# Decoder block with routed experts: results added to token rows block by block, all dense groups ahead of the expert blocks

## The chip, the cores and the metric

One core of a Trainium2 chip runs the whole layer. A core has five engines that run their own instruction streams and meet at semaphores: TensorE (PE, matrix products and transposes), VectorE (DVE), ScalarE (ACT), GpSimd (POOL), and SyncE (SP), which here only issues DMAs. GpSimd issues DMAs too, those that gather or scatter rows by an index. The metric is device time in microseconds, the median of three runs; smaller is better.

## The reference, cut to what matters

The input x is 4 sequences of 1024 tokens of 256 numbers, in float32. The layer is a causal linear attention with 16 heads, a cross attention over 77 context rows, and a feed-forward part with one shared network and eight experts. 512 of the tokens (index_b, index_t) go to the experts:

```
x = x + linear_attention(layernorm(x))
x = x + cross_attention(layernorm(x), ctx)
h = layernorm(x)
shared = ln(silu(h @ sw1.T + sb1) * (h @ sw2.T + sb2)) @ sw3.T + sb3        # all 4096 tokens
h_moe  = h[index_b, index_t]                                              # 512 tokens
e      = argmax(sigmoid(h_moe @ eg_w.T + eg_b) + exp_bias)
w      = softmax([sigmoid(h_moe @ sg_w.T + sg_b), score of e])
y      = ln(silu(h_moe @ ew1[e].T + eb1[e]) * (h_moe @ ew2[e].T + eb2[e])) @ ew3[e].T + eb3[e]
shared[index_b, index_t] = shared[index_b, index_t] * w[0] + y * w[1]
out = x + shared
```

## The kernel before, in words

The 4096 tokens are 32 tiles of 128 (NT), in 8 groups of 4 (NG, GT). A loop of 36 steps does both attentions, tile by tile, in a software pipeline; each finished tile of x is also stored to a scratch tensor in DRAM called rows. The loop's last steps already begin with the feed-forward part.

The feed-forward part goes by units, in the order of the tuple UNITS (L43): F0 to F4, G0, F5, F6, M0, M1, M2, F7. An F unit is a dense group, four tiles through the shared network. G is the gathered group, the 512 tokens that go to the experts, fetched by index from rows and sent through the shared network, for their share of it and for the routing. M units are the experts' blocks: the 512 tokens are sorted by expert into 11 blocks of 128 rows (NBLK), each with rows of one expert only, the last rows of an expert's blocks empty; M0 and M1 have four blocks, M2 three. Every engine runs the loop `for q in range(3, ...)`, and does in step q parts of units q-2 to q+2: on TensorE the gate products of unit q (L688), the transposes of its gated features z for unit q-1 (L721), the input transposes of unit q+1 (L661), and the output products y of unit q-1 (L739). With q = GATHERED = 5 stands G, with FIRST_M = 8 stands M0.

Around the change the order is this.

- GpSimd scatters the normalized gathered tokens into the sorted area of rows (L1666, q = 5) by slot_u; SP loads the blocks back (L441). It also does half of the dense groups' normalizations (norm_h3, L1545), adds the output bias to a whole dense group (bias_tiles, L1560, 128x1024), and computes inverse deviations (invert_variance, L1570; invert_blocks, L1583).
- VectorE writes the gated features (gated, L1231: first an instruction over two SBUF operands, L1235, then one with a PSUM operand, L1240), takes their variances, and evicts y (y_evict, L1210): an F unit is added to x, which SP stores to the output; of an M unit's blocks two are copied by VectorE and two by ScalarE (L989) into ys, and SP stores them to rows (store_ys, L429).
- For the gathered tokens VectorE computes the mixing weights (weigh, L1390, q = 6; weights, L1398, q = 7), then g_a = x + w[0] * shared (add_shared, L1405), to which it adds w[1] * eb3[e] (add_expert_bias, L1410) in q = 8 and 9, from products that TensorE makes (gathered_bias, L796).
- At the end GpSimd gathers the 512 results from rows by slot (L1673), VectorE adds w[1] * result to g_a (add_expert, L1418), and, once every dense group is stored to the output (out_stored), GpSimd scatters the four tiles over it (L1677).

Of the kernel before, what the change touches and what calls it, by code (L numbers as in the profile page):

```python
# [13 lines left out]
P = 128  # L14
# [29 lines left out]
         + tuple(("M", k) for k in range(NMG)) + (("F", NG - 1),))  # L44
# [5 lines left out]
BIAS_ROWS = 64 + NE  # L50

# [6 lines left out]
def decoder_block(nc, A):  # L58
    ctx = ExitStack()
    with ctx:  # L60
# [115 lines left out]
        def qkc(slot, ch):  # L176
# [25 lines left out]
        ys = wide_[:, 2816:5632].rearrange("p (b d) -> p b d", b=NBLK)  # L202
        g_x2, g_sh, hg, g_a = (wide_[:, n:n + 1024].rearrange("p (m d) -> p m d", m=MT)
                               for n in (5632, 6656, 7680, 11264))
        m_th, m_u, m_z = (wide_[:, n:n + 512].rearrange("p (j n) -> p j n", j=GT) for n in (9728, 10240, 10752))
        g_ys, g_out = x[:, 0:MT, :], x[:, MT:2 * MT, :]
        zeros = sb("zeros", [P, D])
# [84 lines left out]
        elog_done, oht_ready, mth_ready, mzt_ready, pair_exp, hg_scaled, ys_copied = (  # L292
            sem(f"act_g_{n}") for n in ("elog", "oht", "mth", "mzt", "pair", "hg", "ys"))
        (idx_ready, cols_ready, g_stat, g_agg, logit_ready, gate_chain, onehot_ready, pair_ready,
         rank_read, slot_ready, block_ready, mu_ready, mz_ready, mstat_done, mzmv_ready, mzn_ready, ys_ready, gsh_ready,
         ga_ready, gb_ready, gout_ready) = (
            sem(f"dve_g_{n}") for n in ("idx", "cols", "stat", "agg", "logit", "gate", "onehot", "pair",
                                        "rank_read", "slot", "block", "mu", "mz", "mstat", "mzmv", "mzn", "ys", "gsh",
                                        "ga", "gb", "out"))
# [4 lines left out]
        ys_stored = sem("ys_stored")  # L304
        gathered = sem("gathered")
        gathered_ys = [sem(f"gathered_ys{m}") for m in range(MT)]
# [11 lines left out]
        ys_v = rows_2[(NT + NBLK) * P:(NT + 2 * NBLK) * P, :].rearrange("(b p) d -> p b d", p=P)  # L318
        to_hs = rows_2[0:(NT + NBLK) * P, :]
        from_ys = rows_2[0:(NT + 2 * NBLK) * P, :]  # L320
# [43 lines left out]
        def _(sp):  # L364
# [52 lines left out]
            load(hs_v, zeros[:, :].unsqueeze(1).to_broadcast([P, NBLK, D]), zeroed)  # L417
# [11 lines left out]
            def store_ys(k):  # L429
                b = blocks_of(k)  # L430
                sp.wait_ge(ys_ready, 2 * (k + 1))
                sp.wait_ge(ys_copied, min(2 * (k + 1), NBLK - 2 * NMG))
                sp.dma_start(ys_v[:, b.start:b.stop, :], ys[:, b.start:b.stop, :]).then_inc(ys_stored, 16)

            for n, (what, k) in enumerate(UNITS):

                if n == 3:
                    sp.wait_ge(placed, 16 * MT)
                    for m in range(NMG):
                        b = blocks_of(m)  # L440
                        sp.dma_start(hs_in[:, b.start:b.stop, :], hs_v[:, b.start:b.stop, :]).then_inc(hs_loaded[m], 16)  # L441
                if what == "F":
                    store_out(k)
                if what == "M":
                    store_ys(k)
            sp.wait_ge(out_stored, 16 * (NG + 1))
            sp.wait_ge(scattered, 16 * MT)
# [3 lines left out]
        def _(pe):  # L451
# [287 lines left out]
            def y_products(pe, n, expert=None):  # L739
                if not 0 <= n < NU:  # L740
                    return
                if is_dense(n):
                    wait(pe, x1_ready, NT)
                    wait(pe, den_ready, NG)
                    wait(pe, ktok_ready, NT)
                    wait(pe, pt_ready, NT)
                    wait(pe, z_ready, dense(n) + 1)
                else:
                    wait(pe, mzt_ready, UNITS[n][1] + 1)
                wait(pe, out_ready, GT * ahead(n, "F"))  # L750
                wait(pe, gsh_ready, GT * ahead(n, "G"))
                wait(pe, ys_ready, 2 * ahead(n, "M"))
                wait(pe, ys_copied, min(2 * ahead(n, "M"), NBLK - 2 * NMG))
# [81 lines left out]
            for q in range(3, NU + 1):  # L835
                if q == FIRST_M - 1:
                    pe.wait_ge(block_ready, 1)
                for half in range(2):
                    gate_products(pe, q, half, expert, load_expert if FIRST_M - 1 <= q < NU - 1 else None)
# [14 lines left out]
        def _(act):  # L854
# [133 lines left out]

            def evict_ys(n):  # L989
                if is_moe(n):  # L990
                    for j in range(2, size(n)):
                        wait(act, y_done, rows_ahead(n) + size(n))
                        copy(ys[:, GT * UNITS[n][1] + j, :], bank[2][:, (j % 2) * D:(j % 2 + 1) * D]).then_inc(ys_copied, 1)

# [31 lines left out]
            for q in range(3, NU + 1):  # L1026
                evict_ys(q - 2)
# [18 lines left out]
        def _(dve):  # L1046
# [307 lines left out]
            def choose_slots():  # L1354
# [17 lines left out]
                dve.tensor_scalar(slot_y[:, :], slot_f[:, :], float(NBLK * P), None, ALU.add).then_inc(slot_ready, 1)  # L1372
# [25 lines left out]
            def weights():  # L1398
                dve.wait_ge(pair_exp, 1)
                then_wait(dve.tensor_reduce(pair_sum[:, :], pair_e[:, :, :], mybir.AxisListType.X, ALU.add))  # L1400
                then_wait(dve.reciprocal(pair_r[:, :], pair_sum[:, :]))
                then_wait(dve.tensor_tensor(mix[:, :, :], pair_e[:, :, :],
                                            pair_r[:, :].unsqueeze(2).to_broadcast([P, MT, 2]), ALU.mult))

            def add_shared(m):  # L1405
                dve.wait_ge(gsh_ready, m + 1)
                dve.scalar_tensor_tensor(out=g_a[:, m, :], in0=g_sh[:, m, :], scalar=mix[:, m, 0:1], in1=g_x2[:, m, :],
                                         op0=ALU.mult, op1=ALU.add).then_inc(ga_ready, 1)

            def add_expert_bias(half):  # L1410
                dve.wait_ge(gbe_done, half + 1)
                for j in range(2):
                    m = 2 * half + j
                    dve.wait_ge(ga_ready, m + 1)
                    dve.scalar_tensor_tensor(out=g_a[:, m, :], in0=bank[3][:, j * D:(j + 1) * D], scalar=mix[:, m, 1:2],
                                             in1=g_a[:, m, :], op0=ALU.mult, op1=ALU.add).then_inc(gb_ready, 1)

            def add_expert(m):  # L1418
                dve.wait_ge(gathered_ys[m], 16)
                dve.wait_ge(gb_ready, m + 1)  # L1420
                dve.scalar_tensor_tensor(out=g_out[:, m, :], in0=g_ys[:, m, :], scalar=mix[:, m, 1:2], in1=g_a[:, m, :],
                                         op0=ALU.mult, op1=ALU.add).then_inc(gout_ready, 1)
# [43 lines left out]
            for q in range(3, NU + 2):  # L1466
# [18 lines left out]
                if q in (FIRST_M, FIRST_M + 1):  # L1485
                    add_expert_bias(q - FIRST_M)
            for m in range(MT):
                add_expert(m)
# [3 lines left out]
        def _(pool):  # L1492
# [129 lines left out]
            pool.memset(zeros[:, :], 0.0)  # L1622
# [27 lines left out]
            for q in range(3, NU + 1):  # L1650

                if q == GATHERED - 2:
# [7 lines left out]
                elif q == GATHERED:  # L1660
# [14 lines left out]
            for m in range(MT):  # L1675
# [61 lines left out]
```

## Time and profile before

| | before |
|---|---|
| median of 3 runs | 413.1 us (413.07 to 413.27) |
| the profiled execution | 412.16 us, of which 410.4 us are the span that the profile shows |
| busy TensorE / VectorE / ScalarE / GpSimd | 375.3 / 299.5 / 166.2 / 252.1 us |
| mean granted clock of TensorE | 0.986 of full speed |
| attention loop, about | 40 to 300 us |
| feed-forward units, about | 300 to 397 us |
| from TensorE's last product to the end of the span | 396.5 to 410.4 us |

The span is the time between the first and the last instruction or transfer of one execution. Busy times of different engines overlap, so that they don't add up to it. What bounds a stretch is read from who waits for whom in that stretch.

### The profile page before, as it was taken

Reading aid. Unit: us, or ns where it says so; the run is one execution under the profiler, and the core shown is the slowest. Engines: PE = TensorE matmul, PEld = TensorE weight load, DVE = VectorE, ACT = ScalarE, POOL = GpSimd, SP = SyncE. Lnnn points to the kernel's source line nnn. Section 1 sums busy time; section 2 is a strip of 40 time slices with the busy share of each in tenths; the row PEclk is TensorE's granted clock in tenths of the full one; section 3 lists DMA queues with packets and bytes.
Section 4 is the critical chain, followed back from the end, with each engine's and each line's share of the span. In section 5 each row is a group of like instructions: output and inputs, shape, how many; then the busy total and the mean of one; then the engine's idle time right before and its main releaser. Section 6 shows DMA issues by size and latency. Waiting matters only on the chain. (4 is left out here: it accounts for less than half of the span.)

```text
span 410.4 us, 11152 instructions
## 1 busy us (share of the span) xinstructions
PE 375.3 (91%) x3826; PEld 259.3 (63%) x3826; DVE 299.5 (73%) x930; ACT 166.2 (41%) x401; POOL 252.1 (61%) x382
## 2 busy tenths in 40 slices
PE   7989899999999999999999999999799979979950
PEld 3455567766776777767767666677566646567630
DVE  2646778888878888888887788785654667988641
ACT  3171343454355344435335424433365443234410
POOL 5133855666656665676656676588788776823435
PEclk9999999999999999999999999999999999999995
DMA  7982591300210120030020012012000320353233
GB/s 225 336 263 51 130 340 53 66 27 14 44 39 25 24 60 14 16 79 15 15 58 22 28 28 53 15 30 65 28 14 27 109 96 2 110 186 103 68 102 126
DMA packets 35743, 31.88 MB, mean 78 GB/s; under 512 B 4027, under 2 KB 34632, under 8 KB 35688
## 3 DMA queue, kind: packets, MB, share of 16 engines
q1 hardware_dynamic: 33160, 26.42, 22.6%
q0 software_dynamic: 1120, 3.36, 2.8%
q10 hardware_dynamic: 1408, 1.39, 1.0%
q8 instruction: 32, 0.52, 0.6%
q14 instruction: 23, 0.19, 0.1%
HBM read 14.64 MB, written 12.32 MB: 66 GB/s over the span
## 5 line engine op out<-in xcount | busy, mean ns | idle before, releaser
L1515 POOL TENSOR_TENSOR s_t<-s_t,causal 128x512 f32<-128x512 f32 x64 | 80.2, 1274 | 75.5 <-ACT s_t L856 75.5
L465 PE MATMUL bank<-h1t,w_qkv 128*128 128x512 f32 x112 | 55.4, 617 | 1.0 <-DVE x L1101 0.8
L1137 DVE TENSOR_TENSOR s_t<-sbank,causal 128x512 f32<-128x512 f32 x64 | 40.8, 678 | 0.0
L472 PE MATMUL bank<-w_qkv,h1t 128*128 128x256 f32 x128 | 35.9, 403 | 2.3 <-DVE arena L1057 2.2
L856 ACT ACTIVATE s_t<-sbank 128x512 f32<-128x512 f32 x64 | 34.2, 587 | 9.1 <-PE sbank L486 9.1
L526 PE MATMUL bank<-s_t,vp 128*32 128x128 f32 x1024 | 34.6, 275 | 2.5 <-DVE s_t L1137 0.9
L486 PE MATMUL sbank<-arena 32*128 32x256 f32 x512 | 36.7, 400 | 0.0
L1101 DVE TENSOR_TENSOR x<-bank,x 128x256 f32<-128x256 f32 x32 | 13.6, 424 | 30.2 <-PE bank L605 30.1
L698 PE MATMUL sbank<-h1t,w 128*128 128x512 f32 x72 | 33.0, 596 | 0.5 <-ACT h1t L856 0.5
L605 PE MATMUL bank<-w_out,attn_t 128*128 128x256 f32 x128 | 33.1, 381 | 0.0
L1523 POOL TENSOR_TENSOR rr<-ve,neg_half 128x3 f32<-128x3 f32 x36 | 31.0, 861 | 3.0
L526 PEld LDWEIGHTS bank<-s_t,vp 128*32 128x32 f32 x1024 | 26.3, 109 | 9.7 <-issue 9.7
L1123 DVE BATCH_NORM_STATS2 stats<-x 128x6 f32<-128x256 f32 x87 | 31.6, 412 | 0.5 <-issue 0.5
L912 ACT ACTIVATE prob<-sc,nmx 128x77 f32<-128x77 f32 x32 | 11.5, 360 | 48.0 <-DVE nmx L1157 48.0
L465 PEld LDWEIGHTS bank<-h1t,w_qkv 128*128 128x128 f32 x112 | 19.0, 189 | 18.1 <-issue 13.7
L856 ACT ACTIVATE prob_t<-bank 77x128 f32<-77x128 f32 x32 | 8.7, 272 | 50.8 <-PE bank L453 50.8
L1057 DVE TENSOR_SCALAR arena<-bank,b_qk 128x512 f32<-128x512 f32 x28 | 21.0, 750 | 11.3 <-PE bank L465 11.3
L856 ACT ACTIVATE k_tok<-bank 128x256 f32<-128x256 f32 x32 | 12.2, 383 | 40.8 <-PE bank L453 40.8
L472 PEld LDWEIGHTS bank<-w_qkv,h1t 128*128 128x128 f32 x128 | 21.8, 189 | 8.8 <-DVE arena L1057 6.7
L486 PEld LDWEIGHTS sbank<-arena 32*128 32x128 f32 x512 | 23.1, 184 | 3.9 <-issue 2.4
L453 PE MATMUL bank<-ident,h 128*128 128x128 f32 x128 | 24.0, 273 | 1.6 <-ACT h L863 1.5
L1534 POOL TENSOR_TENSOR x<-x,b_out 128x256 f32<-128x256 f32 x32 | 23.4, 730 | 0.0
(215 smaller groups left out, 809.7 us busy)
## 6 DMA issues: line engine op xcount, KB each, us to landing
rden_t<-rden SPq DMA_DIRECT2D x64, 64.0 KB
rows<-x SPq DMA_DIRECT2D x32, 128.0 KB, 1.7
x<-in_x SPq DMA_DIRECT2D x7, 512.0 KB, 7.4
out<-x SPq DMA_DIRECT2D x7, 512.0 KB
we<-in_we SPq DMA_DIRECT2D x1, 2048.0 KB
rows<-zeros SPq DMA_DIRECT2D x1, 1408.0 KB, 7.1
xmask<-in_mask POOLq DMA_DIRECT2D x2, 616.0 KB, 7.9
we<-in_we SPq DMA_DIRECT2D x1, 1024.0 KB
```

The costliest lines, as they stand in the source:

```text
L453: return pe.transpose(dst, src, ident[:, :])
L465: mm = pe.matmul(dst[:, :], w_qkv[:, ch, cb * P:(cb + 1) * P], h1t[:, g % 3, ch, :], start=(ch == 0), stop=(ch == CH - 1))
L472: mm = pe.matmul(bank[0][:, 0:D], h1t[:, (t // GT) % 3, ch, tok(t)], w_qkv[:, ch, 2 * D:3 * D], start=(ch == 0), stop=(ch == CH - 1))
L486: mm = pe.matmul(both, kt(slot, ch)[rows, tok(t)], qpair(slot, ch)[rows, :, tok(t)], start=True, stop=True)
L526: mm = pe.matmul(bank[3][32 * r:32 * r + 32, ch * P:(ch + 1) * P], v_of, s_t[:, r, 2 * ch + par, :], start=(first and ch + par == 0), stop ...
L605: mm = pe.matmul(bank[0][:, 0:D], attn_t[:, M % 2, ch, :], w_out[:, ch, :], start=(ch == 0), stop=(ch == CH - 1))
L698: mm = pe.matmul(sbank[2 + half][:, :], w_12[:, ch, half * HF:(half + 1) * HF], h3t[:, n % 2, ch, :], start=(ch == 0), stop=(ch == CH - 1))
L856: return act.activation(dst, src, ACT.Copy)
L1123: last = dve.bn_stats(stats[:, k, :], x[:, t, :])
L1137: dve.tensor_tensor(s_t[:, r, :, :], sbank[r][:, :].rearrange("p (s q) -> p s q", s=4), causal[:, :].unsqueeze(1).to_broadcast([P, 4, P]), ...
L1515: pool.tensor_tensor(s_t[:, r, :, :], s_t[:, r, :, :], causal[:, :].unsqueeze(1).to_broadcast([P, 4, P]), ALU.mult)\
L1523: pool.tensor_tensor(rr[:, i, :], ve[:, i, :], neg_half[:, 0:3], ALU.pow).then_inc(rr_ready, 1)
```

## The change

The dense group F7 goes ahead of the experts' blocks in UNITS, so that M0, M1 and M2 come last (FIRST_M is now 9, and M2 is unit 11). The experts' results no longer go through DRAM. Instead the sums g_a (x plus the shared part plus the expert's bias), with two more columns, the token's weight w[1] and its index in the output, are scattered by GpSimd into a sorted area of rows with 258 columns (place_bases, behind q = 8), which SP had filled beforehand, during tile 16, with zeros and an index out of range (NOWHERE). SP loads them back by unit into res (load_base, behind F7's output store). VectorE then evicts y as res = y * weight + res, all four blocks itself, and GpSimd scatters each block from res to the output by the index column, with a bounds test that skips the empty rows (scatter_blocks, one unit's blocks at the head of steps 11, 12 and 13). The step q = 6 on GpSimd has an order of its own: inverse deviation of G, then the bias of F5 and F6. The experts' bias is added in q = 7 and 8.

```diff
-         + tuple(("M", k) for k in range(NMG)) + (("F", NG - 1),))
+         + (("F", NG - 1),) + tuple(("M", k) for k in range(NMG)))
+BW = D + 2
+BASE_AT = -(-(NT + NBLK) * P * D // BW)
+NOWHERE = 2 * NB * S
             for t in range(NT):
                 if t % GT == 1 and t // GT + 1 < NG:
                     spread(t // GT + 1)
+                if t == 2 * TPB:
+                    load(base_v, empty[:, :].unsqueeze(1).to_broadcast([P, NBLK, BW]), emptied)
-            def store_ys(k):
+            def load_base(k):
                 b = blocks_of(k)
-                sp.wait_ge(ys_ready, 2 * (k + 1))
-                sp.wait_ge(ys_copied, min(2 * (k + 1), NBLK - 2 * NMG))
-                sp.dma_start(ys_v[:, b.start:b.stop, :], ys[:, b.start:b.stop, :]).then_inc(ys_stored, 16)
+                sp.wait_ge(based, 16 * MT)
+                sp.dma_start(res[:, b.start:b.stop, :], base_v[:, b.start:b.stop, :]).then_inc(base_loaded[k], 16)
@@ tensor
-                if q in (FIRST_M, FIRST_M + 1):
-                    gathered_bias(pe, q - FIRST_M)
+                if q in (GATHERED + 2, GATHERED + 3):
+                    gathered_bias(pe, q - GATHERED - 2)
@@ scalar
-                evict_ys(q - 2)
@@ vector, y_evict
+                if is_moe(n):
+                    k = UNITS[n][1]
+                    b = blocks_of(k)
+                    dve.wait_ge(base_loaded[k], 16)
+                    dve.tensor_copy(token_u[:, b.start:b.stop], res[:, b.start:b.stop, D + 1]).then_inc(token_ready, 1)
-                    elif j < 2:
-                        dve.tensor_copy(ys[:, GT * UNITS[n][1] + j, :], y).then_inc(ys_ready, 1)
+                    else:
+                        b = GT * UNITS[n][1] + j
+                        dve.scalar_tensor_tensor(out=res[:, b, 0:D], in0=y, scalar=res[:, b, D:D + 1], in1=res[:, b, 0:D],
+                                                 op0=ALU.mult, op1=ALU.add).then_inc(ys_ready, 1)
@@ vector, weights
+                dve.tensor_copy(g_a[:, :, D], mix[:, :, 1]).then_inc(meta_ready, 1)
+                dve.tensor_copy(g_a[:, :, D + 1], idx_f[:, :]).then_inc(meta_ready, 1)
@@ vector, add_expert and its calls are gone; add_expert_bias in q of 7 and 8
@@ gpsimd
+            def place_bases():
+                pool.wait_ge(emptied, 16)
+                pool.wait_ge(meta_ready, 2)
+                for m in range(MT):
+                    pool.wait_ge(gb_ready, m + 1)
+                    pool.indirect_dma_start(out=to_base, out_offset=bass.IndirectOffsetOnAxis(slot_y[:, m:m + 1], 0),
+                                            in_=g_a[:, m, :], in_offset=None).then_inc(based, 16)
+            def scatter_blocks(n):
+                if is_moe(n):
+                    k = UNITS[n][1]
+                    pool.wait_ge(token_ready, k + 1)
+                    pool.wait_ge(out_stored, 16 * (NG + 1))
+                    for b in blocks_of(k):
+                        pool.wait_ge(ys_ready, b + 1)
+                        pool.indirect_dma_start(out=A["out"], out_offset=bass.IndirectOffsetOnAxis(token_u[:, b:b + 1], 0),
+                                                in_=res[:, b, 0:D], in_offset=None, bounds_check=NB * S - 1,
+                                                oob_is_err=False).then_inc(scattered, 16)
-            for q in range(3, NU + 1):
+            for q in range(3, NU + 2):
+                scatter_blocks(q - 2)
...
                                                 in_=hg[:, m, :], in_offset=None).then_inc(placed, 16)
+                elif q == GATHERED + 1:
+                    norm_h3(q + 2)
+                    invert_variance(q - 1)
+                    bias_tiles(q)
                     bias_tiles(q + 1)
                 else:
                     at(q)
-            pool.wait_ge(ys_stored, 16 * NMG)
-            for m in range(MT):
-                gather(m, g_ys, from_ys, slot_y, gathered_ys[m])
-            pool.wait_ge(out_stored, 16 * (NG + 1))
-            for m in range(MT):
-                pool.wait_ge(gout_ready, m + 1)
-                pool.indirect_dma_start(out=A["out"], out_offset=bass.IndirectOffsetOnAxis(idx_u[:, m:m + 1], 0),
-                                        in_=g_out[:, m, :], in_offset=None).then_inc(scattered, 16)
+                if q == GATHERED + 3:
+                    place_bases()
```

## Rows read from the trace of the kernel before

**Rows 1.** Stretches: from:to, length, busy time (and count) per engine, clock, DMA, GB/s
```profile
400.00:405.00 5.00, 0.00 (x0) 0.00 (x0) 1.85 (x4) 0.00 (x0) 3.46 (x4) 0.50 0.60 188
```

**Rows 2.** Chain that ended last, from 396 us: start, length, what
```profile
398.76 3.91 DMA out<-x
```

**Rows 3.** Timeline of GpSimd, the tail: start, length, instruction [idle before, releaser]
```profile
397.17 1.07 POOL L1601 DMA_INDIRECT x<-rows,slot_y  x1 [0.20 <-issue]
...
404.24 1.09 POOL L1677 DMA_INDIRECT out<-x,idx_u  x1 [0.30 <-issue]
405.64 0.97 POOL L1677 DMA_INDIRECT out<-x,idx_u  x1 [0.30 <-issue]
406.91 0.97 POOL L1677 DMA_INDIRECT out<-x,idx_u  x1 [0.30 <-issue]
```

**Rows 4.** Timeline of TensorE, from the gathered group on
```profile
359.78 1.06 PE L453 MATMUL sbank<-ident,arena 128*128 128x128 f32 x8 [1.15 <-DMA arena<-rows]
362.43 1.97 PE L759 MATMUL bank<-w_3c,s_t 128*128 128x256 f32 x8 [1.59 <-DVE arena L1226]
...
371.27 1.13 PE L800 MATMUL bank<-be,onehot_t 8*128 8x256 f32 x4
...
378.10 1.99 PE L759 MATMUL bank<-we,s_t 128*128 x8 [0.30 <-ACT s_t L999]
...
387.56 3.60 PE L698 MATMUL sbank<-h1t,w 128*128 128x512 f32 x8
390.99 0.49 PE L453 MATMUL bank<-ident,arena 128*128 128x128 f32 x3
...
394.54 1.97 PE L759 MATMUL bank<-w_3c,s_t 128*128 128x256 f32 x8 [0.21 <-ACT arena L856]
```

**Rows 5.** Timeline of VectorE, the same stretch
```profile
348.48 0.19 DVE L1369 TENSOR_TENSOR place<-place,onehot 128x32 f32<-128x32 f32 x1
...
355.08 4.06 DVE L1391 TENSOR_TENSOR oh_score<-onehot,score 128x32 f32<-128x32 f32 x1
...
360.63 1.66 DVE L1226 SCALAR_TENSOR_TENSOR arena<-bank,z_r,y_bias 128x256 f32<-128x256 f32 x4 [0.67 <-POOL z_r L1581]
362.20 0.68 DVE L1235 SCALAR_TENSOR_TENSOR s_t<-s_t 128x512 f32<-128x512 f32 x1
362.97 0.75 DVE L1240 SCALAR_TENSOR_TENSOR s_t<-sbank,b,s_t 128x512 f32<-128x512 f32 x1
...
365.29 1.67 DVE L1407 SCALAR_TENSOR_TENSOR arena<-arena,mix 128x256 f32<-128x256 f32 x4
...
375.25 1.19 DVE L1271 TENSOR_SCALAR arena<-arena,g_zmv,m_r 128x128 f32<-128x128 f32 x4
```

**Rows 6.** Timeline of GpSimd, from the gathered group on
```profile
354.43 4.65 POOL L1567 TENSOR_TENSOR x<-x,y_bias 128x1024 f32<-128x1024 f32 x2
359.17 0.23 POOL L1574 TENSOR_SCALAR z_ve<-z_mv 128x4 f32<-128x4 f32 x1
359.48 1.04 POOL L1581 TENSOR_TENSOR z_r<-z_ve,neg_half 128x4 f32<-128x4 f32 x1
...
387.00 0.86 POOL L1591 TENSOR_TENSOR m_r<-m_ve,neg_half 128x3 f32<-128x3 f32 x1
```

**Rows 7.** Timelines of GpSimd and VectorE near 298 and 305 us
```profile
298.63 0.55 POOL L1529 TENSOR_SCALAR h<-x,nm,rr 128x256 f32<-128x256 f32 x1
...
305.35 1.06 POOL L1529 TENSOR_SCALAR h<-x,nm,rr 128x256 f32<-128x256 f32 x1
...
305.45 0.69 DVE L1235 SCALAR_TENSOR_TENSOR s_t<-s_t 128x512 f32<-128x512 f32 x1
```

**Rows 8.** DMA: the block loads' issues in ns, their time to landing, and the issues' table
```profile
L441 SPq DMA_DIRECT2D arena<-rows x3: 367/507/508, 355.9 to 356.8; - x3
...
DMA to landing us min/median/max: 3.8/4.8/6.2
...
rows<-zeros SPq DMA_DIRECT2D x1, 1408.0 KB, 7.1
```

More of the change, by code:

```diff
@@ L201, in decoder_block @@
         hs_in = wide_[:, 0:2816].rearrange("p (b d) -> p b d", b=NBLK)
[L202 to L207, printed above, removed]
+        res = wide_[:, 2816:2816 + NBLK * BW].rearrange("p (b d) -> p b d", b=NBLK)
+        g_x2, g_sh, hg = (wide_[:, n:n + 1024].rearrange("p (m d) -> p m d", m=MT) for n in (5632, 6656, 7680))
+        g_a = wide_[:, 8704:8704 + MT * BW].rearrange("p (m d) -> p m d", m=MT)
+        m_th, m_u, m_z = (wide_[:, n:n + 512].rearrange("p (j n) -> p j n", j=GT) for n in (9792, 10304, 10816))
+        empty = sb("empty", [P, BW])
+        token_u = sb("token_u", [P, NBLK], U32)
         ones16 = sb("ones16", [P, P], BF16)
@@ L291, in decoder_block @@
             sem(f"pe_g_{n}") for n in ("logit", "rank", "oht", "mxa", "mztr", "gbe"))
-        elog_done, oht_ready, mth_ready, mzt_ready, pair_exp, hg_scaled, ys_copied = (
-            sem(f"act_g_{n}") for n in ("elog", "oht", "mth", "mzt", "pair", "hg", "ys"))
+        elog_done, oht_ready, mth_ready, mzt_ready, pair_exp, hg_scaled = (
+            sem(f"act_g_{n}") for n in ("elog", "oht", "mth", "mzt", "pair", "hg"))
         (idx_ready, cols_ready, g_stat, g_agg, logit_ready, gate_chain, onehot_ready, pair_ready,
          rank_read, slot_ready, block_ready, mu_ready, mz_ready, mstat_done, mzmv_ready, mzn_ready, ys_ready, gsh_ready,
-         ga_ready, gb_ready, gout_ready) = (
+         ga_ready, gb_ready, meta_ready, token_ready) = (
             sem(f"dve_g_{n}") for n in ("idx", "cols", "stat", "agg", "logit", "gate", "onehot", "pair",
                                         "rank_read", "slot", "block", "mu", "mz", "mstat", "mzmv", "mzn", "ys", "gsh",
-                                        "ga", "gb", "out"))
+                                        "ga", "gb", "meta", "token"))
         h3_pooled, g_ve, g_nr, hg_ready, mve_ready, mr_ready = (
@@ L303, in decoder_block @@
         hs_loaded = [sem(f"hs_loaded{k}") for k in range(NMG)]
-        ys_stored = sem("ys_stored")
         gathered = sem("gathered")
-        gathered_ys = [sem(f"gathered_ys{m}") for m in range(MT)]
+        emptied, based = sem("emptied"), sem("based")
+        base_loaded = [sem(f"base_loaded{k}") for k in range(NMG)]
         scattered = sem("scattered")
@@ L416, in _ @@
             load(idx_t[:, :], A["idx_t"], w_moe_in)
-            load(hs_v, zeros[:, :].unsqueeze(1).to_broadcast([P, NBLK, D]), zeroed)
+            load(hs_v, empty[:, 0:D].unsqueeze(1).to_broadcast([P, NBLK, D]), zeroed)
             for t in range(NT):
@@ L444, in _ @@
                 if what == "M":
-                    store_ys(k)
+                    load_base(k)
             sp.wait_ge(out_stored, 16 * (NG + 1))
-            sp.wait_ge(scattered, 16 * MT)
+            sp.wait_ge(scattered, 16 * NBLK)
         @block.tensor
@@ L751, in y_products @@
                 wait(pe, gsh_ready, GT * ahead(n, "G"))
-                wait(pe, ys_ready, 2 * ahead(n, "M"))
-                wait(pe, ys_copied, min(2 * ahead(n, "M"), NBLK - 2 * NMG))
+                wait(pe, ys_ready, min(GT * ahead(n, "M"), NBLK))
                 for j in range(size(n)):
@@ L838, in _ @@
                 for half in range(2):
-                    gate_products(pe, q, half, expert, load_expert if FIRST_M - 1 <= q < NU - 1 else None)
+                    gate_products(pe, q, half, expert, load_expert if FIRST_M - 1 <= q < NU else None)
                 z_features(pe, q - 1)
@@ L986, in gates @@
                     act.activation(m_th[:, own, :], x1, ACT.Tanh, scale=0.5).then_inc(mth_ready, 1)
[L989 to L993, printed above, removed]
             def evict_z(n):
@@ L1371, in choose_slots @@
                 dve.tensor_copy(slot_u[:, :], slot_f[:, :]).then_inc(slot_ready, 1)
-                dve.tensor_scalar(slot_y[:, :], slot_f[:, :], float(NBLK * P), None, ALU.add).then_inc(slot_ready, 1)
+                dve.tensor_scalar(slot_y[:, :], slot_f[:, :], float(BASE_AT - NT * P), None, ALU.add)\
+                    .then_inc(slot_ready, 1)
             def map_blocks():
@@ L1403, in weights @@
                                             pair_r[:, :].unsqueeze(2).to_broadcast([P, MT, 2]), ALU.mult))
+                dve.tensor_copy(g_a[:, :, D], mix[:, :, 1]).then_inc(meta_ready, 1)
+                dve.tensor_copy(g_a[:, :, D + 1], idx_f[:, :]).then_inc(meta_ready, 1)
             def add_shared(m):
                 dve.wait_ge(gsh_ready, m + 1)
-                dve.scalar_tensor_tensor(out=g_a[:, m, :], in0=g_sh[:, m, :], scalar=mix[:, m, 0:1], in1=g_x2[:, m, :],
+                dve.scalar_tensor_tensor(out=g_a[:, m, 0:D], in0=g_sh[:, m, :], scalar=mix[:, m, 0:1], in1=g_x2[:, m, :],
                                          op0=ALU.mult, op1=ALU.add).then_inc(ga_ready, 1)
@@ L1414, in add_expert_bias @@
                     dve.wait_ge(ga_ready, m + 1)
[L1415 to L1422, printed above, removed]
+                    dve.scalar_tensor_tensor(out=g_a[:, m, 0:D], in0=bank[3][:, j * D:(j + 1) * D], scalar=mix[:, m, 1:2],
+                                             in1=g_a[:, m, 0:D], op0=ALU.mult, op1=ALU.add).then_inc(gb_ready, 1)
             def first_stats_of(lo, hi):
@@ L1621, in _ @@
             pool.memset(one1[:, :], 1.0)
-            pool.memset(zeros[:, :], 0.0)
+            pool.memset(empty[:, 0:BW - 1], 0.0)
+            pool.memset(empty[:, BW - 1:BW], float(NOWHERE))
             pool.memset(vp[:, :, :, :], 0.0)
```

11 lines of the change are left out of this document (5 added, 6 removed).

## The prediction, made before the changed kernel was run

> **What bounds the kernel now.** I read the stretches first, then the chain of waits, then the engines' timelines from 350 us on. Up to 396 us TensorE is hardly ever idle; from 400 to 405 it does nothing and the DMA share is 0.60 [rows 1]. The span therefore ends with a tail that no matmul covers. The last dense group's store holds it for 3.91 us [rows 2], and GpSimd issues four gathers and four scatters by index, each 0.96 to 1.09 us and 0.30 us apart [rows 3]. The last scatter ends at 407.88 and the span at 410.4, so its landing costs 2.5. Ahead of the tail, TensorE waits twice in the gathered group's neighbourhood: 1.15 us for the sorted tokens, and 1.59 us for the vector engine [rows 4].
>
> The second of these waits has a cause one engine further on. A 128x32 product on VectorE takes 4.06 us at 355.08, while one of the same shape and both operands in SBUF takes 0.19 at 348.48 [rows 5]. It ends at 359.14, where GpSimd's two 128x1024 bias sums end (354.43 + 4.65 = 359.08) [rows 6]. Only then can the mixing weights go on.
>
> **The change, part by part.** Times below are on the clock of the profiled execution: its span is 410.4, 1.76 more lie around it (412.16), and the median of the runs is 0.94 above that (413.1).
>
> *Tail removed.* Gone are three stores of results, four gathers, four final sums and four scatters to the output. After TensorE's last product (396.5) they and the last group's evictions took 13.9 us to the end.
>
> *F7 moved ahead of the blocks.* Its TensorE work is the same: 3.43 us of gate products (387.56 to the next at 390.99), 1.98 of output products [rows 4], 1.3 of transposes, 6.7 in all. The blocks start that much later unless idle time goes. The 1.15 us wait for sorted tokens goes: F7's transposes now stand there, and their input (two GpSimd normalizations, 0.55 each [rows 7], behind the placement scatters, after which GpSimd is free at 354.4 [rows 6]) is ready at 355.5.
>
> *GpSimd's order.* The gathered group's inverse deviation now goes ahead of the bias sums: ready at 355.5 + 0.09 + 0.20 + 0.08 + 1.04 = 356.9, where it was 360.5 [rows 6]. The group's four evictions (1.66 [rows 5]) end at 358.6 instead of 362.2, so the 1.59 us wait goes too. Were that all, 2.7 us of TensorE's idle time would go.
>
> But the bias sums are now three in a row (F5, F6 and, because F7 has moved up, F7), 2.35 each: 356.9 to 363.9. At 358.6 VectorE comes to the gate's first product of unit 7, 128x512 with both inputs in SBUF. The row at 355.08 says what such an instruction does when it meets back-to-back bias sums: it waited through the rest of both. The hold works the other way too: a 0.55 us normalization on GpSimd took 1.06 while VectorE's product of that form ran [rows 7]. So I let it wait until 363.9, then 0.68 + 0.75 [rows 5] gives z at 365.4.
>
> The Trainium skill, "SBUF — State Buffer", section "SBUF: two separate sides", says that GpSimd and a VectorE instruction with two SBUF inputs exclude each other over a shared port pair, and whichever starts first keeps it for the whole instruction. By that rule alone the product would get in after the first or second sum (359.3 or 361.6); the trace's 4.06 us shows a wait over two.
>
> From there, unit by unit (VectorE in program order):
> - VectorE: z 365.4; variance of unit 6 to 366.4; weights and the two new small copies to 367.3 (0.57 before, 0.3 taken for the copies, from the 0.16 to 0.19 of small instructions); four sums of the shared part to 368.9 (1.67); half of the experts' biases 0.8 (halves of the 1.66 rows) to 369.7; F5 out 1.6 to 371.3 [rows 5].
> - TensorE: y of unit 6 from 359.4, bias products 1.06 to 362.3, then waits 3.1 for z; F7's gates 365.4 to 368.9; transposes; waits 1.1 for F5 out; y 371.4 to 373.2, bias products to 374.2. M0's gates start at 374.2, which was 364.2 before: 10.0 later, 3.3 more than F7's 6.7.
> - M0 as before, 8.2 without the wait, then the last dense group's variance (after M0's, as in the program) ends at 381.6; GpSimd's two inverses (1.4, 1.3 [rows 6]) put F7's scale at 383.0 and M0's at 384.3; F7 is out at 384.6, M0's normalization ends at 385.8 (1.19 [rows 5]), and 1.74 later, as before (376.36 to 378.10 [rows 4]), its y products run to 389.5. M2's gates end at 392.6, 8.2 later than before.
>
> *The experts' bias* is added two units earlier, so g_a is ready at 375.1. Four placement scatters follow at 1.27 (0.97 + 0.30 [rows 3]): 375.2 to 380.3, landed by 383. Queued behind them on GpSimd is the inverse for F7, which wants nothing before 381.6: hidden, by 1.3 us.
>
> *Emptying the base rows* during tile 16 is a 1.45 MB store; the like one landed in 7.1 us [rows 8]. The tile after it stores its rows a whole tile step (8.4 us) later and nobody waits for those: nothing, and at worst about 1 us once. The second memset (0.1) lies in GpSimd's idle 1.1 us at the start: nothing.
>
> *Base rows back to SBUF.* Nothing like this load stood in the tail. SP issues it behind F7's store: 384.7 + two issues of 0.5 = about 385.2. Lower bound 3.8, upper 6.2 to landing for the three comparable loads, median 4.8 [rows 8]; 3.91 for a 256 KB store in contention [rows 2]. I take 5.0, as 512 KB of store are ahead: 390.2. M0's products are done at 389.5, so this load holds by 0.7, and could hold by 2.
>
> *Evictions and scatters.* VectorE: a small copy and 0.45, first block at 390.8; GpSimd starts at 391.1. Now 11 scatters instead of four, with a bounds test and rows skipped: no row shows one. Bounds: the skipped rows (896 of 1408) may cost nothing, 0.3 + 0.35 x 0.97 = 0.65 each; the test may add to the slowest spacing 1.40 (404.24 to 405.64 [rows 3]); 1.6 is my estimate of the most, one and a half times as far above that as it is above 1.27. I take 1.27, the spacing of plain ones. M0's four end at 396.2; M2's inverse is queued behind them (0.20 + 0.08 + 0.86 + gaps = 1.2; its input is there at 395.6) to 397.4; seven more to 406.3, of which the last 0.3 is gap. M2's own results are evicted from 400.9 on, before its scatters' turn at 402.5. End: 406.0 + 2.5 = 408.5, against 410.4: 1.9 saved. So 410.3 for a profiled execution, 411.2 for the median.
>
> **The rivals.**
> (B) VectorE gets in between bias sums. At 361.6 everything behind is 2.1 us earlier: 409.1; if it is never held, M0 starts 4.1 earlier: 407.1. For: the 0.09 us gap ahead of a small GpSimd instruction let VectorE in at 359.1 [rows 6], and the third sum comes from another step of the program. Against: two sums already ran without such a gap.
> (C) Scatters get cheap with their skipped rows. At 0.65 the tail is no longer GpSimd's; it is gates of M2 (392.6) + 8.3 to the first eviction + three scatters + landing: about 405.6, so 408.3.
> (D) Slower: the bounds test costs more than skipped rows give. GpSimd's queue holds 11 scatters in a row on the path, so each 0.1 costs 1.1. From 1.27 + 1.9/11 = 1.44 there is no gain, above 1.52 it is slower; at 1.6 it is 3.6 more: 414.8. For: 1.40 has been seen among plain ones, and these are issued behind waits. Against: most rows move nothing.
> (E) The base load lands 2 us later behind F7's store (6.2 and more instead of 5): 413.1, no change. This is also how the edit could fail to do what it says: one wait for a DMA replaced by another.
>
> **How the numbers follow.** Forecast 0.45 (411.2, by itself 409.7 to 412.6), B 0.18, C 0.12, D 0.15, E 0.10. The range reaches from B's end to short of D's: 406.8 to 414.0. What this kernel's measurement can tell from no change is 0.2%, 0.8 us. Faster is below 412.3: most of the forecast's case (0.39), B, C: 0.69. Same: the forecast's rest 0.05, most of E, D's edge: 0.14. Slower: D and some of E: 0.17.
>
> **What would show it.** In the trace after: three bias sums end near 364 and a 128x512 product on VectorE takes about 5.3 us; if it takes 0.7, B. TensorE starts M0's gates at 374. A load of base rows lands within 1 us of M0's last product. Eleven output scatters 1.27 apart (C, D by their spacing), the first at 391, and after TensorE's last product (401) about 7.5 us to the end instead of 13.9. The forecast is wrong if the product isn't held, if the spacing is not near 1.27, or if GpSimd's queue is not what ends last.

## The result, and the profile after

The changed kernel takes 410.01 us (median of 20 runs, 407.03 to 413.65) beside 414.95 for the kernel before (20 runs, 411.46 to 416.9, the first three of which are those shown ahead of the prediction). The ratio is 0.988, with an interval of 0.985 to 0.991: 5.0 us faster (3.8 to 6.3). The forecast was 411.2 with 1.9 us saved. The time lies in the range, but the saving is more than twice the forecast one. That 410.01 comes so near to 411.2 is in part luck: the forecast stood on 413.1, the median of three runs of the kernel before, and over 20 runs that median is 1.9 higher.

In the profiled executions the span went from 410.4 to 406.6 us. Executions of one kernel differ ahead of the stretch that was changed (last section), so I compare traces by what comes after one instruction that no edit touches: the start of TensorE's output products of unit 5, the gathered group, at 352.79 before and 353.02 after. Put on the clock of the trace before, the span after is 406.6 - 0.23 = 406.4, 4.0 us less.

TensorE's timeline after, from the gathered group on:

```profile
358.70 1.04 PE L460 MATMUL sbank<-ident,h1t 128*128 128x128 f32 x8
359.57 1.89 PE L765 MATMUL bank<-w_3c,s_t 128*128 128x256 f32 x8
361.39 1.12 PE L806 MATMUL bank<-be,onehot_t 8*128 8x256 f32 x4
362.45 3.70 PE L705 MATMUL sbank<-h1t,w 128*128 128x512 f32 x8
...
369.11 1.96 PE L765 MATMUL bank<-w_3c,s_t 128*128 128x256 f32 x8 [1.65 <-DVE x L1226]
371.00 1.12 PE L806 MATMUL bank<-be,onehot_t 8*128 8x256 f32 x4
372.06 1.13 PE L718 MATMUL sbank<-we,h1t 128*128 x4
```

Both waits of [rows 4] in this stretch (1.15 and 1.59 us) are gone, and F7's gates follow at 362.45 without a wait, where the forecast had 3.1 us of idleness. One wait of 1.65 us is new, for F5's evictions. M0's gates start at 372.06; the forecast said 374.2.

VectorE and GpSimd in the same stretch, two fences that answer to [rows 5] and [rows 6]:

```profile
355.32 0.15 DVE L1397 TENSOR_TENSOR oh_score<-onehot,score 128x32 f32<-128x32 f32 x1
...
357.32 1.66 DVE L1229 SCALAR_TENSOR_TENSOR arena<-bank,z_r,y_bias 128x256 f32<-128x256 f32 x4 [0.86 <-POOL z_r L1581]
358.90 1.21 DVE L1240 SCALAR_TENSOR_TENSOR s_t<-s_t 128x512 f32<-128x512 f32 x1
...
362.32 2.33 DVE L1408 TENSOR_TENSOR mix<-pair_e,pair_r 128x8 f32<-128x8 f32 x1
...
367.20 1.65 DVE L1226 SCALAR_TENSOR_TENSOR x<-bank,z_r,x 128x256 f32<-128x256 f32 x4
```

```profile
356.18 1.04 POOL L1581 TENSOR_TENSOR z_r<-z_ve,neg_half 128x4 f32<-128x4 f32 x1
357.21 7.42 POOL L1567 TENSOR_TENSOR x<-x,y_bias 128x1024 f32<-128x1024 f32 x3
```

The three bias sums stand back to back as forecast (end 364.63). But the gate's first product, which comes at 358.90, takes 1.21 us and not 5.3: it is through at 360.11. The three sums take 7.42 instead of three times 2.35, the second of them 2.80, since it had to wait for the product. The weights' product (8 numbers for each partition), ready at 362.32, is then held through the third sum, 2.33 us instead of the 0.17 that it took before. It came 0.04 us too late; the third sum in the chain of waits:

```profile
362.28 2.34 POOL x L1567
```

A stretch of the chain that ended last, and the timeline of GpSimd's tail, which answers to [rows 2] and [rows 3]:

```profile
383.28 4.32 DMA arena<-rows
387.63 0.04 DVE token_u L1215
```

```profile
389.11 1.05 POOL L1667 DMA_INDIRECT out<-arena,token_u  x1 [0.80 <-DVE arena L1233]
...
394.36 0.88 POOL L1591 TENSOR_TENSOR m_r<-m_ve,neg_half 128x3 f32<-128x3 f32 x1
395.45 1.10 POOL L1667 DMA_INDIRECT out<-arena,token_u  x1 [0.20 <-issue]
...
401.96 0.97 POOL L1667 DMA_INDIRECT out<-arena,token_u  x1 [0.31 <-issue]
403.23 0.97 POOL L1667 DMA_INDIRECT out<-arena,token_u  x1 [0.30 <-issue]
```

The load of M0's base rows (first fence) takes 4.32 us and lands at 387.60, when M0's products are done (385.53 + 1.99 = 387.5). The 11 scatters are 1.27 to 1.40 apart, but for M2's inverse between the first four and the rest. The last is issued by 404.20 and its landing takes 2.4.

### The profile page after: what moved, and what is told of

Read it like the earlier page. It is cut to its first block and busy times, and to the rows that moved or that the text cites. A ratio compares the mean times of both kernels' runs of the same rounds, so it can differ in the third digit from the quotient of the medians.

```text
span 406.6 us, 11163 instructions
## 1 busy us (share of the span) xinstructions
PE 375.4 (92%) x3826; PEld 259.2 (64%) x3826; DVE 298.8 (73%) x936; ACT 164.8 (41%) x396; POOL 259.6 (64%) x390
```

## Experiments

The aligned span in the table is the profiled span less the delay of unit 5's output products against 352.79. h1_small_product has no ratio: it was executed once, as were h2_small_between and h3_product_later, which are told of below. The other ratios rest on 6 to 20 runs of a kernel.

| run | edit | span | aligned | ratio to before (95% interval) |
|---|---|---|---|---|
| before | | 410.4 | 410.4 | |
| after | the change | 406.6 | 406.4 | 0.988 (0.985 to 0.991) |
| c0_changed | the change again | 408.4 | 406.6 | 0.990 (0.984 to 0.995) |
| u1_units_only | before, F7 ahead of the blocks | 418.7 | 416.7 | 1.014 (1.010 to 1.018) |
| p1_inverse_first | before, GpSimd's new step 6 | 410.0 | 408.3 | 0.992 (0.989 to 0.995) |
| b1_bias_late, b2 | after, F7's bias sum late | 404.4, 406.1 | 404.3, 404.3 | 0.985 (0.981 to 0.990), 0.986 (0.980 to 0.992) |
| n1_no_skip | after, all rows written | 408.4 | 406.4 | 0.989 (0.983 to 0.994) |
| t1_seven | after, without M0's scatters | 405.2 | 405.2 | 0.986 (0.980 to 0.992) |
| h1_small_product | after, one product more | 406.2 | 406.2 | |
| f1_bias_late_base_first, f2 | b1, base rows first | 408.7, 405.7 | 403.8, 403.9 | 0.980 (0.975 to 0.985), 0.987 (0.981 to 0.993) |

**The change again (c0_changed).** No edit.

> The changed kernel once more, beside the others: about 0.988 of the kernel before. Its trace tells whether the 4.06 us hold of a small two-input product on VectorE and the short waits of the changed kernel (1.21 and 2.33 us for instructions of 0.68 and 0.17) come out alike in every execution. If VectorE gets in between two bias sums by chance, the numbers differ from run to run; if it depends on the order of the instructions, they repeat.

The holds repeat to 0.01 us: 1.22 and 2.33. The third sum starts 0.04 us ahead of the weights' product here too (363.90 and 363.94). So they come from the program, the order of its instructions and their times, and not from chance.

**The order of the units alone (u1_units_only).**

```diff
 # before.py
-         + tuple(("M", k) for k in range(NMG)) + (("F", NG - 1),))
+         + (("F", NG - 1),) + tuple(("M", k) for k in range(NMG)))
-                    gate_products(pe, q, half, expert, load_expert if FIRST_M - 1 <= q < NU - 1 else None)
+                    gate_products(pe, q, half, expert, load_expert if FIRST_M - 1 <= q < NU else None)
-            for q in range(3, NU + 1):        # ScalarE, for evict_ys
+            for q in range(3, NU + 2):
```

> The kernel before with F7 moved ahead of the blocks and nothing else. Theory 1 (the gain needs the results' new way to the output): slower than before by about 3 us, since store of M2's results (2.5 to landing), four gathers (1.27 apart, 3.6 to landing), four sums and four scatters now all stand behind TensorE's last product with nothing beside them: last product near 397, end near 413. Theory 2 (the order of the dense groups alone brings the gain, by the idle 1.15 us and 1.59 us on TensorE): 2 to 3 us faster than before.

Slower by 1.4%, 6.3 us in the aligned span: theory 1's sign, at twice its size. The end is what it says, one after the other. The chain of waits from 403 us:

```profile
403.43 2.51 DMA rows<-arena
...
406.22 1.06 POOL x L1601
...
411.35 1.00 POOL out L1677
...
415.22 0.97 POOL out L1677
```

The rest of its loss is in the gathered group. GpSimd now has F7's normalizations between its two bias sums, and the small product is held through all of them:

```profile
357.12 5.14 DVE L1391 TENSOR_TENSOR oh_score<-onehot,score 128x32 f32<-128x32 f32 x1
```

```profile
356.47 2.35 POOL L1567 TENSOR_TENSOR x<-x,y_bias 128x1024 f32<-128x1024 f32 x1
358.80 1.09 POOL L1557 TENSOR_SCALAR h1t<-x,nm,rr 128x256 f32<-128x256 f32 x2
359.87 2.34 POOL L1567 TENSOR_TENSOR x<-x,y_bias 128x1024 f32<-128x1024 f32 x1
```

TensorE then waits 4.01 us where it waited 1.59 before. So the order of the units is not a gain by itself: in the changed kernel it pays together with the results' new way and GpSimd's new order. What it would bring with only one of them was not run.

**GpSimd's order of step 6 alone (p1_inverse_first).**

```diff
 # before.py
+                elif q == GATHERED + 1:
+                    norm_h3(q + 2)
+                    invert_variance(q - 1)
+                    bias_tiles(q)
+                    bias_tiles(q + 1)
```
(the bias sum of F5 goes from step 5 to here)

> The kernel before with only GpSimd's order of step 6 changed (the gathered group's inverse deviation ahead of the two bias sums). Theory 1 (the hold is what TensorE waits for): the small product takes 0.2 us instead of 4.06, the gathered group's evictions end near 359, TensorE's wait of 1.59 us at 362.43 goes and its blocks start 1.6 to 1.8 us earlier; time 1.6 us less. Theory 2 (the tail is set by something that does not move, the store of F7 and the gathers): less than 0.4 us.

```profile
356.76 0.15 DVE L1391 TENSOR_TENSOR oh_score<-onehot,score 128x32 f32<-128x32 f32 x1
```

```profile
362.43 1.89 PE L759 MATMUL bank<-w_3c,s_t 128*128 128x256 f32 x8
```

Theory 1: the small product takes 0.15 us, TensorE's wait of 1.59 is gone, the aligned span is 2.1 us less and the ratio 0.992. By the traces this order alone brings about half of what the change brings (2.1 of 4.0); the two ratios' intervals (0.992, 0.988) meet. The tail does not take it back.

**F7's bias sum late (b1_bias_late, b2_bias_late).**

```diff
 # after.py, GpSimd
+                elif q == GATHERED + 2:
+                    norm_h3(q + 2)
+                    invert_variance(q - 1)
+                    pool.wait_ge(ga_ready, MT)
+                    bias_tiles(q + 1)
```

> The changed kernel with F7's bias sum moved behind the inverse deviation of unit 6 and behind VectorE's sums of the shared part. Theory 1: the weights' product (2.33 us at 362.3) takes 0.17, F5's evictions end near 366.7 instead of 368.8, TensorE's wait of 1.65 us at 369.1 goes and M0's gates start near 370.3; everything behind moves with it, so 1.6 to 2 us less than the changed kernel. Theory 2: the bias sum in its new place holds another VectorE instruction with two SBUF inputs (the gate's first product of unit 8) for as long, and nothing is won.

> The changed kernel with the late bias sum, again, beside the next one on one chip: 2 us less than the changed kernel, 0.985 to 0.987 of the kernel before.

VectorE of b1_bias_late, and TensorE's start of M0:

```profile
362.20 0.17 DVE L1408 TENSOR_TENSOR mix<-pair_e,pair_r 128x8 f32<-128x8 f32 x1
...
364.94 1.64 DVE L1226 SCALAR_TENSOR_TENSOR x<-bank,z_r,x 128x256 f32<-128x256 f32 x4
366.50 0.72 DVE L1240 SCALAR_TENSOR_TENSOR s_t<-s_t 128x512 f32<-128x512 f32 x1
```

```profile
370.04 1.13 PE L718 MATMUL sbank<-we,h1t 128*128 x4
```

The product is no longer held (0.17), M0 starts 2.0 us earlier (1.9 aligned) and the end comes 2.1 us earlier in both traces. Against the changed kernel the ratios (0.985 and 0.986, beside 0.988 and 0.990) point the same way, but their intervals overlap. The third sum ahead of this work was on the path; theory 2 is out, as the gate's product at 366.50 took 0.72. But the edit moves two things: with the hold goes the wait of F5's inverse deviation behind that sum, which F5's evictions need (ready at 366.19 before the edit, at 363.59 with it). Had only the hold gone, the evictions would have started near 366.2 instead of 367.2, by my estimate from these rows. So about 1 us of the 2.1 is the hold's alone, and the rest needs the earlier inverse too.

**No row skipped (n1_no_skip).** Every scatter writes its 128 rows to a scratch tensor of its own; the experts' tokens are missing from the output.

```diff
 # after.py
-                        pool.indirect_dma_start(out=A["out"], ...
-                                                in_=res[:, b, 0:D], in_offset=None, bounds_check=NB * S - 1,
-                                                oob_is_err=False).then_inc(scattered, 16)
+                        pool.indirect_dma_start(out=A[f"dump{b}"], ...
+                                                in_=res[:, b, 0:D], in_offset=None).then_inc(scattered, 16)
```
(the empty rows' index column holds 4096 plus 1 to 128, by partition)

> The changed kernel with no bounds test and no row skipped: each of the 11 scatters writes all its 128 rows, to a scratch tensor of its own in DRAM instead of the output (left out: the experts' tokens in the output). Theory 1 (GpSimd builds 128 entries whatever their index, so skipping saves it nothing): spacing stays 1.28, the tail lasts as long, time within 0.5 us of the changed kernel. Theory 2 (skipped rows are cheap, the test dear, and they happen to cancel): the spacing moves by at least 0.1, the time by 1 us or more.

```profile
400.57 0.96 POOL L1672 DMA_INDIRECT dump<-arena,token_u  x1 [0.30 <-issue]
402.16 0.96 POOL L1672 DMA_INDIRECT dump<-arena,token_u  x1 [0.63 <-issue]
403.43 0.96 POOL L1672 DMA_INDIRECT dump<-arena,token_u  x1 [0.30 <-issue]
```

0.96 us a scatter against 0.97 with the test. Rivals C (0.65 us apart) and D (1.44 and more) were out by the changed kernel's own spacing of 1.27. This run adds that the test and the 896 skipped rows together change GpSimd's time by 0.01 us. It can't tell nothing from a cost and a saving that cancel, but the changed kernel's trace can. These are its stretches of M0's scatters and of M2's, and this run's of M2's (columns as in [rows 1]):

```profile
389.10:394.00 4.90, 3.95 (x20) 2.64 (x17) 4.16 (x18) 1.44 (x3) 3.97 (x4) 1.00 0.23 71
400.65:406.60 5.95, 0.00 (x0) 0.00 (x0) 0.00 (x0) 0.00 (x0) 2.92 (x3) 0.50 0.02 0
```

```profile
402.10:408.40 6.30, 0.00 (x0) 0.00 (x0) 0.13 (x1) 0.00 (x0) 2.88 (x3) 0.50 0.23 83
```

M2's three scatters moved next to nothing in the changed kernel (0 GB/s, where this run moves 83), M0's moved data (71 GB/s), and both take 0.97 to 0.98 us each, apart from the first of a burst. So skipped rows save GpSimd nothing, and the test costs it at most 0.02 us (M0's later three 0.98, 0.98 and 0.97 in the changed kernel, 0.97, 0.96 and 0.96 in this run).

The scatter at 402.16 is M2's first, and it came 0.33 late (0.63 idle instead of 0.30). M2's own products took 2.92 us here, at a granted clock of 0.50 from 399 to 401, and 1.89 in the changed kernel, where the clock was 0.92 from 397 to 399. So M2's evictions began only at 400.90; M0's first scatter, too, stands 1.28 behind the start of its evictions (389.07), and 400.90 + 1.28 is 402.2. The aligned span hides this delay: VectorE, which the later stretch waits for, was 1.69 us behind the trace before (unit 5's products 1.99), and aligned by it the span is 406.7, 0.3 more than the changed kernel's.

**Without M0's four scatters (t1_seven).** M0's tokens are missing from the output.

```diff
 # after.py
-                    for b in blocks_of(k):
+                    for b in (blocks_of(k) if k else ()):
```

> The changed kernel without the four scatters of M0 (left out: those tokens in the output). Theory 1 (GpSimd's queue ends last, but only 1.5 us ahead of the chain over M2's own results): the four scatters are 5.1 us of GpSimd's time, yet only about 1 to 1.5 us are won, since M2's inverse then starts 1.1 us earlier and M2's chain sets the end. Theory 2 (the tail is a plain sum of scatters): 5.1 us less.

```profile
397.96 1.27 DVE L1233 SCALAR_TENSOR_TENSOR arena<-bank,arena 128x256 f32<-128x256 f32 x3 [2.54 <-PE bank L765]
```

```profile
394.25 1.05 POOL L1667 DMA_INDIRECT out<-arena,token_u  x1 [0.31 <-DVE arena L1233]
```

1.2 us less, not 5.1: theory 1. The first of the seven is issued at 394.25, when M1's results and M2's inverse (393.95) are there. M2's own evictions (397.96) come only just ahead of their turn (399.47), since a scatter that waits for its evictions stands 1.4 us behind their start (389.11 and 387.70 in the changed kernel). GpSimd's queue ends last in the changed kernel, but a second chain, over M2's variance and inverse, runs 1.2 us behind it.

**Which instruction gets a turn (h1, h2, h3).** One small product more, ahead of the gate's product of unit 7:

```diff
 # after.py, VectorE
+                    if n == GATHERED + 2:
+                        dve.tensor_tensor(spare[:, :, :], onehot[:, :, :], score[:, :, 0:NE], ALU.mult)
```

> The changed kernel with one more product on VectorE, 128x32 with both inputs in SBUF (the same one that was held for 4.06 us before, into a spare tile), put directly ahead of the gate's first product of unit 7, that is into the stretch of the three bias sums. Theory 1 (a small instruction finds no turn between back-to-back sums, a large one does): it takes about 5 us, to the end of the third sum, and M0's gates start 2 us or more later. Theory 2 (whichever has waited gets in at the next boundary, whatever its size): it ends with the first sum, after about 0.7 us, and the gate's product follows without a hold or waits for one sum.

```profile
358.70 0.71 DVE L1242 TENSOR_TENSOR spare<-onehot,score 128x32 f32<-128x32 f32 x1
359.33 2.88 DVE L1243 SCALAR_TENSOR_TENSOR s_t<-s_t 128x512 f32<-128x512 f32 x1
```

Theory 2: the small one gets in at the end of the first sum, and the large one is then held for the second. The size does not decide. The weights' product was not held here (0.17 at 364.42), yet the aligned span is only 0.2 less than the changed kernel's: in both, VectorE gets past that product only when the third sum has ended. That left open why an equal product was held through two sums before. Two edits of the kernel before:

```diff
 # before.py, GpSimd, between the placement scatters and the bias sums (h2)
+                    pool.tensor_scalar(spare[:, :], g_mv[:, :, 0], -1.0, 1.0, ALU.mult, ALU.mult)
 # before.py, VectorE, ahead of the small product (h3)
+                for n in range(3):
+                    dve.bn_stats(spare[:, n, :], x[:, 0, :])
```

> The kernel before with one small GpSimd instruction (128x4, into a spare tile) between the last placement scatter and the two bias sums. In the kernel before, VectorE's small product was held through both sums; in the changed kernel, where a small instruction stands ahead of the sums, an equal product got in at the first boundary. Theory A (what runs on GpSimd ahead of the sums decides): the product is now held for 2 us at most, to the end of the first sum. Theory B (when the product comes decides, or the instruction ahead of it on VectorE): 4 us again.

> The kernel before with three statistics of 256 numbers (0.41 us each, into a spare tile) ahead of the small product, so that it comes 1.2 us later into the first bias sum (at about 1.9 us of 2.35 instead of 0.65). Theory B (its time of arrival decides): it gets in at the end of the first sum, about 0.6 us. Theory A (what runs on GpSimd ahead of the sums decides): held to the end of the second, about 2.9 us.

VectorE of h2_small_between, then VectorE and GpSimd of h3_product_later:

```profile
356.91 1.94 DVE L1392 TENSOR_TENSOR oh_score<-onehot,score 128x32 f32<-128x32 f32 x1
358.89 2.25 DVE L1393 COPY pair<-score 128x4 f32<-128x4 f32 x1
```

```profile
360.71 3.10 DVE L1394 TENSOR_TENSOR oh_score<-onehot,score 128x32 f32<-128x32 f32 x1
```

```profile
359.10 4.65 POOL L1570 TENSOR_TENSOR x<-x,y_bias 128x1024 f32<-128x1024 f32 x2
```

Theory A. With a 0.19 us instruction on GpSimd ahead of the two sums (356.47 to 361.11) the product was through at 358.85, the end of the first; the copy behind it was held for the second instead. Without it, coming later did not help (3.10, to the end of the second at 363.75). Over these traces it is one pattern: where the series of GpSimd's elementwise instructions directly follows the indirect DMAs, the hold lasts to the end of the series (4.06, 5.14, 3.10; in the second, the normalizations are part of the series); where a small instruction stands between, VectorE gets in at the next boundary (1.21, 1.22, 0.71, 1.94). The 3.10 and the 1.94 are of one execution each. Why that is so is open.

**The base rows ahead of F7's store (f1, f2).** With the late bias sum as well.

```diff
 # after.py, SP
                 if what == "F":
+                    if k == NG - 1:
+                        load_base(0)
                     store_out(k)
-                if what == "M":
+                if what == "M" and k:
                     load_base(k)
```

> The changed kernel with F7's bias sum late, as in the run before, and with M0's base rows loaded ahead of F7's output store instead of behind it. Theory 1: VectorE no longer waits for the base rows; M0's first eviction starts when its product and VectorE are free, about 1 us earlier, and since GpSimd's queue of 11 scatters begins there, the end comes 1 us earlier than with the late bias sum alone, 3 us before the changed kernel. Theory 2: F7's store, which every scatter waits for, now lands later and holds the first scatter instead: nothing more than the late bias sum gives.

> Late bias sum and base rows first, again. By the first trace M0's scatters start 0.4 to 0.8 us earlier than with the late bias sum alone, so 0.3 to 1 us less than that kernel. If the larger distance of the first measurement (0.9796 against 0.9854) was real, it is 2 us or more less.

Inconclusive in the times: 0.980 on one chip, 0.987 beside 0.986 for b2 on another. The two traces agree on 0.4 us less than with the late bias sum alone (403.8 and 403.9 against 404.3), less than expected. GpSimd of f2:

```profile
387.01 1.01 POOL L1593 TENSOR_TENSOR m_r<-m_ve,neg_half 128x4 f32<-128x4 f32 x1
388.20 1.06 POOL L1669 DMA_INDIRECT out<-arena,token_u  x1 [0.18 <-issue]
```

VectorE reaches M0's results at once, but the first scatter now waits for M1's inverse ahead of it on GpSimd and starts 0.5 us earlier (aligned) than with the late bias sum alone. From there to the end of the last scatter it is 15.1 us in all four traces (after, b1, f1, f2), so the end moves by that and no more. M2's evictions come barely in time for their turn (401.38 and 402.80 in f1). This kernel is the shortest by trace; its two ratios both lie below 1 by more than their intervals, but they do not set it apart from b1.

## Why the prediction was right, and where its size was off

Of the three signs that would have made the forecast wrong, one came in part: GpSimd's queue ended last and the spacing was 1.27, but the gate's product was held for 0.5 us and not for 4.6. In this step what came is nearest to rival B.

- *GpSimd's order and the two waits of TensorE.* Right. The gathered group's inverse is there at 357.2 (forecast 356.9), its evictions end at 358.98 (358.6), both waits are gone.
- *Three bias sums hold VectorE.* That GpSimd's sums hold VectorE was right, the step "So I let it wait until 363.9" was not. I took the 4.06 us of [rows 5] for the rule of back-to-back sums. It was the special case of a series directly behind indirect DMAs. The product was let in after the first sum (1.21 us) and the weights' product was held through the third instead (2.33). So this step was charged too much: M0's gates start at 372.06 less 0.23, against 374.2, and everything behind has kept 2 us or more of that distance (F7 out at 382.84, forecast 384.6; first scatter 389.1, forecast 391.1). The span is 2.1 us shorter than the forecast's 408.5. That is rival B's first price, 409.1 us; the profiled execution, 408.39, with the 0.94 us that the forecast put between it and the median, gives 409.3. In part this is luck: B let the gate's product in after the second sum and held nothing else. In h1_small_product the gate's product did wait for the second sum, and the span was 0.2 us from the changed kernel's. The section of the Trainium skill that I weighed against the row, "SBUF — State Buffer", section "SBUF: two separate sides" (whichever starts first keeps the ports for the whole instruction), fits the changed kernel, with 1.21 and 2.33 us; the 4.06, 5.14 and 3.10 us lie outside it.
- *Unit by unit from M0 to M2, M0's base rows, the eviction.* Right within 0.7 us: the load took 4.32 (forecast 5.0), landed 0.1 after M0's products (forecast 0.7) and held VectorE, which was free before them, for 0.69.
- *11 scatters at 1.27, landing 2.5.* Right: from the first scatter to the end of the last 15.1 us (forecast 14.9), landing 2.4. That the bounds test and the skipped rows cost and give nothing was an assumption; the spacing of M0's and M2's scatters and n1_no_skip show it.
- *M2's results in time for their turn.* Right: their evictions began 1.6 us ahead of it in the forecast (400.9, 402.5) and 1.9 us in the trace (398.76, 400.68). The forecast left out that a scatter stands 1.4 us behind the start of its evictions, so only about 0.5 us was to spare.
- *E, the load lands late.* Did not happen.
- *What a measurement can tell from no change, 0.8 us.* Too little: it was taken from three runs within 0.2 us of each other. The 20 runs of the kernel before lie 5.4 us apart, and the interval of the saving is 2.5 us wide.

Of 4.0 us by the traces, 1.9 were forecast and 2.1 are what the forecast charged too much for the three sums. The interval of the timed 5.0 us (3.8 to 6.3) includes 4.0.

## What to carry to other kernels

Before a large elementwise instruction is put on GpSimd, look what VectorE does in that stretch: instructions there whose inputs are all in SBUF, even of 8 numbers for each partition, can wait for it, and the wait is counted as their duration, so that it shows in no list of waits but as one instruction far above its like (2.33 us for 0.17). Here moving one such sum behind VectorE's weights and shared sums was worth 2.1 us by the traces, with the inverse deviation that this brought forward; the rest of the change adds, by subtraction, 1.9 to the 2.1 of GpSimd's new order. And when an order of work is changed, look for the order's second effect (three sums in a row instead of two) on the engine next to it; price a hold by more than one row, since one row may be the special case.

## What the runs showed of the hardware

- A copy of 128x4 with one SBUF source was held by a GpSimd sum too (2.25 us for 0.17, h2_small_between).
- A scatter by index costs GpSimd 0.96 to 0.98 us and 0.30 ahead of the next (the first of a burst 1.05 to 1.10), with 128 rows written (n1_no_skip) or with nearly all skipped (M2's in the changed kernel).
- The 350 us ahead of the changed stretch are not the same in every execution. TensorE's granted clock in the first 40 us was 1.00 in the trace after, 0.96 in c0_changed and 0.91 in f1_bias_late_base_first, and unit 5's output products came 0.2, 1.8 and 4.9 us later than in the trace before. Of f1's delay against the trace after, 3.0 us were there at VectorE's statistics at 289.21 (292.18 in f1) and the other 1.6 came right behind, where f1's clock was 0.83 from 290 to 300 and the trace after had 1.00. By the span alone, f1 (408.7) would have looked slower than the changed kernel (406.6). The windows 0 to 40 us of these three, and 290 to 300 of f1:

```profile
0.00:40.00 40.00, 34.23 (x165) 19.70 (x166) 19.16 (x55) 13.46 (x28) 14.27 (x39) 1.00 0.77 224
```

```profile
0.00:40.00 40.00, 34.01 (x148) 19.03 (x148) 17.68 (x51) 13.34 (x27) 13.19 (x38) 0.96 0.76 224
```

```profile
0.00:40.00 40.00, 33.80 (x113) 18.45 (x114) 17.45 (x49) 13.35 (x27) 11.90 (x36) 0.91 0.77 224
```

```profile
290.00:300.00 10.00, 8.21 (x86) 5.99 (x84) 4.55 (x15) 4.28 (x12) 6.42 (x10) 0.83 0.05 16
```
